# Fire attention in a 12-stage transformer kernel: scores in four 32-row products, projections beside a double-buffered bias stage

## The chip, the cores and the metric

The kernel runs on one core of one Trainium2 chip, as one program. The metric is device time in microseconds from start to end of the execution. Three runs of the kernel before gave 4412.99, 4416.31 and 4423.09 us; their median, 4416.31, is what the change is compared with.

## The reference

The input is 8 sequences of 256 positions and 128 channels. The program puts it through a mixture of experts, a gated recurrence, a second mixture of experts, a 6-layer local transformer, an attention with a position bias called Fire, and a second 6-layer local transformer, each behind a layer normalisation. Only the Fire attention changes. Cut to what it computes, with 16 heads of 8 channels:

```
pos = arange(T);  rel = pos[:, None] - pos[None, :]
pos_norm = log(|c * max(pos, |L| * 512)| + 1) + 1e-6
nd   = log(|c * rel| + 1) / pos_norm[:, None]                    # T x T distances
bias = einsum('tsw,wh->hts', relu(nd[..., None] * w1[0] + b1), w2) + b2   # 32 hidden, 16 heads
bias = where(causal, bias, -inf)
q, k, v = split(x @ Wqkv + bqkv)                                 # 16 heads of 8
att  = softmax(q @ k.T / sqrt(8) + bias)
y    = (att @ v) @ Wproj + bproj;   x = x + y
```

The bias is one table of 16 x 256 x 256 for all 8 sequences.

## The kernel before

`fire_attention_phase` is written with one instruction list for each engine, and semaphores between them; nothing reorders the work, so that an engine takes its list in the order written. It has three blocks, and each ends for all engines before the next begins.

*Setup* (L1364 to L1399): loads of the weights, the relative positions and the like, and the logarithms and the reciprocal that the distances need.

*Bias stage* (L1402 to L1466): the table is made in eight rounds of 32 key positions. A round has eight distance products on DVE (L1416, into `fa_nd`), one Relu of 128x2048 on ACT (L1440, into `fa_hb`), 16 matmuls of 64 columns on PE (L1451; 8 in rounds 4 to 7, where only the second half of the queries can see the keys), and the evacuation with `b2` on DVE (L1424, into `fa_bias`). There is one `fa_nd`, one `fa_hb` and one set of PSUM banks, so that each step of a round waits for the one before. Behind the eighth round GpSimd fills the future positions with -1e30 (L1462).

*Attention* (from L1517): each of the 8 sequences (`b`, two of them in a pass of the loop, told apart by `par`) is split into 12 blocks of 128 queries x 512 columns: four blocks for the first 128 queries (four heads of 128 keys each) and eight for the second 128 (two heads of 256 keys each). 96 blocks run through a pipeline in slots. For a block, PE makes the scores (L1568), DVE adds the bias (L1654) and takes the maximum of a row (L1657), GpSimd subtracts it (L1532), ACT takes the exponential (L1617), PE turns the block by four transposes (L1558), ACT copies it out of PSUM (L1611), and PE weighs the values (L1594). At the end of a tile of 128 queries (after block 4 and block 12) DVE divides by the sum (L1663, L1666), PE turns the result (L1581), ACT copies it (L1621), PE projects it (L1575), ACT adds the bias into `fa_ysb` (L1626) and DVE adds it to `M` (L1673).

Heads have 8 channels, while a matmul contracts over all 128 partitions. The kernel before keeps the keys in `fa_kz`, 16 copies of them, in copy h all channels but those of head h at zero. The copies are made on DVE, four heads at a time (L1643), out of the projection that PE makes at the start of each sequence (L1546, L1550), from a copy of `XN` that GpSimd makes (L1526).

A matmul of float32 shows in the trace as two weight loads (PEld) and two records on PE; a transpose shows as one.

Of the kernel before, what the change touches and what calls it, by code (L numbers as in the profile page):

```python
# [1315 lines left out]
def fire_attention_phase(nc, res, d, M, XN):  # L1316
# [3 lines left out]
    GA, GT = 12, 4  # L1320
    RM = T + 4 * (T // 4 - 1)
    ROFF = RM - T
    with ExitStack() as ctx:
# [16 lines left out]
        hmask = sb("fa_hmask", [P, NH])  # L1340
        rel = sb("fa_rel", [P, RM])
        pn = sb("fa_pn", [P, T])
        nd = sb("fa_nd", [P, 8, T])
        hb = sb("fa_hb", [P, 8, T])
        bias = [sb("fa_bias0", [P, NH, P]), sb("fa_bias1", [P, NH, T])]
        xb = sb("fa_xb", [P, T])
        qT = sb("fa_qT", [P, 2, T])
        kz = sb("fa_kz", [P, 2, NH, T])
        vv = sb("fa_vv", [P, 2, 2, NH, HV])
        S = sb("fa_S", [P, 4, 512])  # L1350
        mx = sb("fa_mx", [P, 4, 4])
        pT = sb("fa_pT", [P, 2, 4, P])
        rd = sb("fa_rd", [P, 2, NH])
        on = sb("fa_on", [P, 2, P])
        oT = sb("fa_oT", [P, P])
        ysb = sb("fa_ysb", [P, 2, P])
        ld, zd, ach, vch = sem("fa_ld"), sem("fa_zd"), sem("fa_ach"), sem("fa_vch")
        ndd, hd_, bp, be = sem("fa_ndd"), sem("fa_hd"), sem("fa_bp"), sem("fa_be")
        SCALE = float(np.float32(1.0) / np.sqrt(np.float32(HD)))


        with nc.Block() as block:
            @block.sync
            def _(sp):  # L1364
                for dst, src in ((wqkv[:, :], d["fa_wqkv"]), (wp[:, :], d["fa_wp"]), (bqk[:, :], d["fa_bqk"]),
                                 (bv[:, :], d["fa_bv"].to_broadcast([P, P])), (b2[:, :], d["fa_b2"].to_broadcast([P, NH])),
                                 (sc[:, 0:2], d["fa_sc"].to_broadcast([P, 2])), (wb[:, :], d["fa_wb"]),
                                 (hmask[:, :], d["c_hmask"]), (rel[:, :], d["c_rel"]), (pn[:, :], d["c_pos"])):
                    sp.dma_start(dst, src).then_inc(ld, 16)
# [5 lines left out]
            @block.gpsimd  # L1375
            def _(pool):
                nc.gpsimd.memset(w2[:, :], 0.0).then_inc(zd, 1)
                nc.gpsimd.memset(vv[:, :, :, :, :], 1.0)
# [21 lines left out]


        with nc.Block() as block:  # L1402
            def rounds(eng, body):
                body(0, 2)
                with eng.Fori(1, 4) as r:
                    body(r, 2)
                with eng.Fori(4, 8) as r:
                    body(r, 1)

            @block.vector  # L1410
            def _(dve):
                def distances(r, tiles):
                    if not isinstance(r, int):
                        dve.wait_ge(hd_, r)
                    for i in range(8):
                        ins = nc.vector.tensor_tensor(nd[:, i, :], rel[:, bass.ds(r * -32 + (ROFF - 4 * i), T)]  # L1416
                                                      if not isinstance(r, int) else rel[:, ROFF - 4 * i:ROFF - 4 * i + T],
                                                      pn[:, :], ALU.mult)
                    ins.then_inc(ndd, 1)

                def evacuate(r, tiles):
                    dve.wait_ge(bp, r + 1)
                    for t in range(2 - tiles, 2):
                        ins = nc.vector.tensor_tensor(bias[t][:, :, bass.ds(r * 32, 32)],  # L1424
                                                      bank[t][:, :].rearrange("p (s h) -> p h s", h=NH),
# [3 lines left out]
                def body(r, tiles):  # L1429
                    distances(r, tiles)  # L1430
                    evacuate(r, tiles)
                rounds(dve, body)

            @block.scalar
            def _(act):
                def body(r, tiles):
                    act.wait_ge(ndd, r + 1)
                    if not isinstance(r, int):
                        act.wait_ge(bp, r)
                    nc.scalar.activation(hb[:, :, :], nd[:, :, :], ACT.Relu, scale=wb[:, 0:1], bias=wb[:, 1:2]).then_inc(hd_, 1)  # L1440
                rounds(act, body)

            @block.tensor
            def _(pe):
                def body(r, tiles):
                    pe.wait_ge(hd_, r + 1)
                    if not isinstance(r, int):
                        pe.wait_ge(be, r)
                    for t in range(2 - tiles, 2):
                        for i in range(8):  # L1450
                            ins = nc.tensor.matmul(bank[t][:, i * 4 * NH:(i + 1) * 4 * NH], hb[:, i, t * P:(t + 1) * P],  # L1451
                                                   w2[:, :], start=True, stop=True, skip_group_check=True)
                    ins.then_inc(bp, 1)
                rounds(pe, body)

            @block.gpsimd
            def _(pool):

                pool.wait_ge(be, 8)
                for t in range(2):  # L1460
                    n = (t + 1) * P
                    nc.gpsimd.affine_select(out=bias[t][:, :, :], in_=bias[t][:, :, :], compare_op=ALU.is_ge, fill=-BIG,  # L1462
                                            base=t * P, pattern=[[0, NH], [-1, n]], channel_multiplier=1)

        simd, addd, mxd, subd, expd = [sem("fa_" + n) for n in ("simd", "addd", "mxd", "subd", "expd")]
        ptT, ptE, pvd = [sem("fa_" + n) for n in ("ptT", "ptE", "pvd")]
        xbd, projd, qE, kzd, vE = [sem("fa_" + n) for n in ("xbd", "projd", "qE", "kzd", "vE")]
        rdd, ond, oTd, oTe, yd, yE, upd = [sem("fa_" + n) for n in ("rdd", "ond", "oTd", "oTe", "yd", "yE", "upd")]  # L1470
        SIM, PTR, PVS, OTR, YPR = 4, 6, 7, 8, 9
        G2 = 2 * GA

        def back(g, k):

# [349 lines left out]
```

## Time and profile before

| | us |
|---|---|
| median of 3 runs | 4416.31 |
| the profiled execution | 4419.39 |
| its span in the trace | 4417.6 |
| PE, DVE, ACT, POOL busy in the span | 3899.8, 3447.6, 3176.4, 2673.5 |
| Fire attention: setup | 12.8 |
| Fire attention: bias stage | 97.2 |
| Fire attention: attention | 299.2 |

The engines are PE (TensorE's matmuls), PEld (its weight loads), DVE (VectorE), ACT (ScalarE), POOL (GpSimd) and SP (SyncE, which starts transfers). [...] Most of the span belongs to the two local transformers (slices 7 to 20 and 26 to 39 of the page's 40). The Fire attention lies between 2307 and 2716 us of the span. The page's chain of waits covers only the last layer normalisation, so that the stage is read from windows and from the timeline.

### The profile page before, as it was taken

How to read it: one execution, taken by the hardware profiler on the slowest of the kernel's cores; microseconds unless marked ns; L12 is line 12 of the kernel's file. 1: busy time of each engine (PE TensorE's matmuls, PEld its weight loads, DVE VectorE, ACT ScalarE, POOL GpSimd, SP SyncE). 2: the span in 40 equal slices, each digit the busy share in tenths (PEclk: the TensorE clock that was granted, in tenths of full speed). 3: DMA queues.
4: the chain of work that ended last, by engine and by line, in shares of the span. 5: the costliest groups of instructions: out<-in, count | busy, mean ns of one | idle time of the engine just before them, and what ended most of it. 6: DMA issues, size and time to landing. Idle time of an engine off the chain costs nothing. (4 is left out here: it accounts for less than half of the span.)

```text
span 4417.6 us, 164417 instructions
## 1 busy us (share of the span) xinstructions
PE 3899.8 (88%) x64144; PEld 2853.1 (65%) x64144; DVE 3447.6 (78%) x6675; ACT 3176.4 (72%) x10347; POOL 2673.5 (61%) x2507
## 2 busy tenths in 40 slices
PE   7966968999999999999954896899999999999996
PEld 3423437777777777777734664777777777777773
DVE  1132129999999999999943664999999999999994
ACT  3343337888888888888841433788888888888884
POOL 1110127777777777777710332777777777877772
PEclk8987989999999999999975987999999999999997
DMA  1101113333333333333310000333333333333341
GB/s 58 57 15 44 57 47 105 115 103 119 100 116 103 106 112 108 114 97 109 117 29 0 1 0 33 103 112 104 119 99 116 104 108 112 103 117 98 106 119 37
DMA packets 549303, 377.81 MB, mean 86 GB/s; under 512 B 32576, under 2 KB 533056, under 8 KB 546240
## 3 DMA queue, kind: packets, MB, share of 16 engines
q1 hardware_dynamic: 548560, 367.57, 27.6%
q8 instruction: 507, 8.31, 0.8%
q14 instruction: 236, 1.93, 0.1%
HBM read 265.37 MB, written 102.11 MB: 83 GB/s over the span
## 5 line engine op out<-in xcount | busy, mean ns | idle before, releaser
L1266 POOL TENSOR_TENSOR lt_t<-lt_t 128x512 f32<-128x512 f32 x768 | 973.5, 1289 | 567.8 <-DVE lt_t L1100 567.8
L1002 ACT ACTIVATE lt_pb<-lt_pb,lt_mx 128x64 f32<-128x64 f32 x3072 | 1023.5, 346 | 0.0
L1272 POOL TENSOR_TENSOR lt_t<-lt_t,lt_rn 128x512 f32<-128x512 f32 x768 | 810.8, 1076 | 118.4 <-DVE lt_rn L1128 117.1
L49 PE MATMUL ps<-lt_wh,lt_xh 128*128 128x512 f32 (+1 forms) x1536 | 581.8, 379 | 148.9 <-DVE lt_t L1100 87.6
L1002 ACT ACTIVATION_READ_ACCUMULATOR lt_pb<-lt_pb,lt_mx 128x1 f32 x3072 | 610.2, 199 | 0.0
L984 ACT ACTIVATE lt_qkT<-ps 128x512 f32<-128x512 f32 x768 | 459.0, 598 | 197.2 <-PE ps L804 196.8
L1111 DVE TENSOR_REDUCE lt_ss<-lt_sq 128x8 f32<-128x512 f32 x768 | 518.7, 675 | 14.5 <-ACT lt_sq L979 9.9
L1100 DVE TENSOR_TENSOR lt_t<-ps,lt_tab 128x512 f32<-128x512 f32 x768 | 522.9, 681 | 2.9
L51 PE MATMUL ps<-lt_wh,lt_xl 128*128 128x512 f32 (+1 forms) x1536 | 523.7, 341 | 0.0
L1106 DVE TENSOR_TENSOR lt_t<-ps,lt_tab 128x512 f32<-128x512 f32 x768 | 521.6, 679 | 1.6 <-PE ps L804 0.3
L50 PE MATMUL ps<-lt_wl,lt_xh 128*128 128x512 f32 (+1 forms) x1536 | 522.8, 340 | 0.0
L804 PE MATMUL ps<-ident,lt_t 128*128 128x128 f32 x3072 | 482.8, 280 | 34.1 <-ACT lt_qkT L984 25.5
L979 ACT ACTIVATE lt_sq<-ps 128x512 f32<-128x512 f32 x768 | 452.8, 590 | 71.4 <-PE ps L51 70.5
L49 PEld LDWEIGHTS ps<-lt_wh,lt_xh 128*128 128x128 f32 x1536 | 290.5, 189 | 267.5 <-issue 150.6
L804 PEld LDWEIGHTS ps<-ident,lt_t 128*128 128x128 f32 x3072 | 355.9, 141 | 159.0 <-issue 105.6
L862 PEld LDWEIGHTS ps<-lt_pT,lt_vw 64*64 64x64 f32 x24576 | 397.1, 135 | 89.0 <-issue 88.7
L862 PE MATMUL ps<-lt_pT,lt_vw 64*64 64x32 f32 x24576 | 439.0, 221 | 4.1 <-issue 3.9
L1278 POOL TENSOR_TENSOR lt_pb<-lt_pb,lt_rd 128x512 f32<-128x512 f32 x384 | 400.8, 1044 | 34.1 <-DVE lt_rd L1145 30.7
L876 PE MATMUL ps<-lt_oT,lt_wo 128*128 128x256 f32 x1536 | 405.1, 386 | 1.8 <-ACT lt_oT L1014 1.4
L372 POOL TENSOR_TENSOR M<-M,moe_tmp 128x512 f32<-128x512 f32 x64 | 81.0, 1266 | 510.5 <-DVE moe_tmp L354 510.5
L354 DVE SCALAR_TENSOR_TENSOR moe_tmp<-ps,moe_bb,moe_cbc 128x512 f32<-128x512 f32 x64 | 48.1, 751 | 419.8 <-PE ps L306 419.8
L832 PEld LDWEIGHTS ps<-lt_qkT 64*32 64x32 f32 x24576 | 271.1, 105 | 139.1 <-issue 136.7
(196 smaller groups left out, 7989.3 us busy)
## 6 DMA issues: line engine op xcount, KB each, us to landing
lt_vw<-v_scratch SPq DMA_DIRECT2D x768, 256.0 KB, 3.7
v_scratch<-lt_vv SPq DMA_DIRECT2D x384, 256.0 KB, 2.1
lt_wraw<-in_lt_wqkv SPq DMA_DIRECT2D x56, 384.0 KB, 5.6
moe_cbc<-comb_scratch SPq DMA_DIRECT2D x16, 1024.0 KB, 6.7
moe_w<-in_moe_w SPq DMA_DIRECT2D x32, 256.0 KB, 2.8
lt_wo<-in_lt_wo SPq DMA_DIRECT2D x48, 128.0 KB, 3.7
lt_w<-in_lt_w SPq DMA_DIRECT2D x12, 341.0 KB, 4.2
lt_w<-in_lt_w SPq DMA_DIRECT2D x12, 192.0 KB, 3.3
```

The source lines that it names most:

```text
L49: nc.tensor.matmul(out, lh, rh, start=start, stop=False)
L50: nc.tensor.matmul(out, lh, rl, start=False, stop=False)
L51: return nc.tensor.matmul(out, ll, rh, start=False, stop=stop)
L804: ins = nc.tensor.transpose(TB[:, q * P:(q + 1) * P], t1[:, u[1] % 2, t, q * P:(q + 1) * P], ident[:, :])
L862: ins = nc.tensor.matmul(OR[r][64 * e:64 * e + 64, t * P + w * WIN:t * P + w * WIN + WIN], vw[h, k, 4 * t + w, e * DH:(e + 1) * DH], pT[h, ...
L984: nc.scalar.activation(qkT[:, u[1] % 2, :, WIN + t * P:WIN + (t + 1) * P], TB.rearrange("p (a n) -> p a n", a=4), ACT.Copy).then_inc(tE[t], 1)
L1002: ins = nc.scalar.activation(p, p, ACT.Exp, bias=mx[:, par, c:c + 1], accum_out=sm[:, par, c:c + 1])
L1100: nc.vector.tensor_tensor(o4, a4[:, :, :, ::-1, :], s4, ALU.mult).then_inc(rotd[t], 1)
L1106: nc.vector.tensor_tensor(t1[:, u[1] % 2, t, :].rearrange("p (w h c) -> p w h c", w=2, c=DH), A[t][:, :].rearrange("p (w h c) -> p w h c", ...
L1111: nc.vector.tensor_reduce(ss[:, u[1] % 2, 8 * t:8 * t + 8], sq[:, t, :].rearrange("p (h c) -> p h c", c=DH), AX.X, ALU.add).then_inc(ssd[t ...
L1266: nc.gpsimd.tensor_tensor(o, o, t2[:, t, :], ALU.add).then_inc(padd[t], 1)
L1272: nc.gpsimd.tensor_tensor(o, o, rn[:, u[1] % 2, 8 * t:8 * t + 8].unsqueeze(2).to_broadcast([P, 8, DH]), ALU.mult).then_inc(qkd[t], 1)
```

## The change

*Heads by groups of 32 rows.* Channels 32r to 32r+31 hold the heads 4r to 4r+3. `fa_kz` now has four copies for each sequence, each with one head of every group of 32 partitions. A product of 32 rows (`scores`, L1560) then gives the scores of the heads of one group; the four of a group of blocks use the four quarters of the array's rows and write banks 0 to 3. Blocks are numbered so that the row group runs fastest; in one group of four blocks, each block has another r. DVE adds the bias of the four blocks one after the other, and then takes the maximum of one block in each slot. `fa_S` has 8 buffers, `fa_pT` 3, and the PSUM banks of the turned weights and of the output move.

*Projections.* All eight sequences are projected in the bias stage, one in each round, straight from `XN`, ahead of the round's products on PE. ACT copies the queries and the keys (`take_queries`), DVE the values, and GpSimd spreads the keys (`spread_keys`). Queries, keys and values of all sequences are kept.

*Bias stage.* `fa_nd`, `fa_hb` and the PSUM banks of the products have two buffers. The causal fill is made in each round for its 32 positions.

*Loops.* All loops are written out, so that waits are on constants.

The diff, cut to its core:

```diff
@@ bias stage @@
+                distances(0)
+                for r in range(8):
+                    if r < 7:
+                        distances(r + 1)
+                    take_values(r)
+                    take_bias(r)
...
             @block.scalar
             def _(act):
-                def body(r, tiles):
-                    act.wait_ge(ndd, r + 1)
-                    if not isinstance(r, int):
-                        act.wait_ge(bp, r)
-                    nc.scalar.activation(hb[:, :, :], nd[:, :, :], ACT.Relu, scale=wb[:, 0:1], bias=wb[:, 1:2]).then_inc(hd_, 1)
-                rounds(act, body)
+                def hidden(r):
+                    act.wait_ge(ndd, r + 1)
+                    if r >= 2:
+                        act.wait_ge(bp, r - 1)
+                    nc.scalar.activation(hb[:, r % 2, :, :], nd[:, r % 2, :, :], ACT.Relu, scale=wb[:, 0:1],
+                                         bias=wb[:, 1:2]).then_inc(hd_, 1)
+
+                def take_queries(b):
+                    act.wait_ge(qkp, b + 1)
+                    nc.scalar.activation(qT[:, b, :], bank[4 + b % 2][:, 0:T], ACT.Identity, bias=sc[:, 3:4],
+                                         scale=SCALE).then_inc(qE, 1)
+                    if b >= 2:
+                        act.wait_ge(kzd, b - 1)
+                    nc.scalar.activation(kT[:, b % 2, :], bank[4 + b % 2][:, T:2 * T], ACT.Identity, bias=bqk[:, 1:2]).then_inc(kE, 1)
+                for r in range(8):
+                    take_queries(r)
+                    hidden(r)
...
+                for r in range(8):
+                    project(r)
+                    biases(r)
...
+                def spread_keys(b):
+                    pool.wait_ge(kE, b + 1)
+                    nc.gpsimd.tensor_tensor(kz[:, b, :, :], kT[:, b % 2, :].unsqueeze(1).to_broadcast([P, GR, T]),
+                                            hmask[:, :].unsqueeze(2).to_broadcast([P, GR, T]), ALU.mult).then_inc(kzd, 1)
@@ attention, PE @@
-                        nc.tensor.matmul(bank[q[1] % 2][:, :].rearrange("p (h k) -> p h k", h=nh),
-                                         qT[:, par, t * P:(t + 1) * P], kz[:, par, h0:h0 + nh, 0:nk],
-                                         start=True, stop=True).then_inc(simd, 1)
+                def scores(q):
+                    if q:
+                        pe.wait_ge(addd, q)
+                    for r in range(GR):
+                        b, _, t, a, nh, nk = info(q + r)
+                        rows = slice(32 * r, 32 * r + 32)
+                        nc.tensor.matmul(bank[r][:, :].rearrange("p (h k) -> p h k", h=nh),
+                                         qT[rows, b, t * P:(t + 1) * P], kz[rows, b, a:a + nh, 0:nk],
+                                         start=True, stop=True).then_inc(simd, 1)
...
+                def slot(n):
+                    q = at(n, PTR)
+                    if q is not None:
+                        turn_weights(q)
+                    q = at(n, SIM)
+                    if q is not None and q % GR == 0:
+                        scores(q)
+                    tl = tile_end(at(n, YPR))
+                    if tl is not None:
+                        project(tl)
+                    tl = tile_end(at(n, OTR))
+                    if tl is not None:
+                        turn_output(tl)
+                    q = at(n, PVS)
+                    if q is not None:
+                        weigh(q)
@@ attention, DVE @@
+                def slot(n):
+                    q = at(n, SIM)
+                    if q is not None:
+                        if q % GR == 0:
+                            for k in range(GR):
+                                add_bias(q + k)
+                        maximum(q)
+                    q = at(n, PVS)
+                    tl = tile_end(q)
+                    if tl is not None:
+                        take_output(q, tl)
+                    tl = tile_end(at(n, YPR))
+                    if tl is not None:
+                        update(tl)
```

The lags are, in slots behind the scores (`SIM`): turning (`PTR`) 2, weighing (`PVS`) 3, turning of the output (`OTR`) 4, its projection and the update of M (`YPR`) 5; between these stages they were the same before.

On ACT, in the bias stage, the rows before are these (the Relu of round 0, of the rounds 1 to 3 in a loop, of 4 to 7 in a loop, and then the first rows of the attention):

```order
L1440 ACTIVATE fa_hb<-fa_nd,fa_wb 128x2048
L1405 UNCONDITIONAL_BRANCH
L1405 ISA
L1440 ACTIVATE fa_hb<-fa_nd,fa_wb 128x2048
L1405 REGISTER_ALU
L1405 COMPARE_AND_BRANCH
```

and after the change (`fa_qT` the queries, `fa_kT` the keys, `fa_hb` the Relu):

```order
L1453 ACTIVATE fa_qT<-ps,fa_sc 128x256
L1457 ACTIVATE fa_kT<-ps,fa_bqk 128x256
L1448 ACTIVATE fa_hb<-fa_nd,fa_wb 128x2048
L1453 ACTIVATE fa_qT<-ps,fa_sc 128x256
L1457 ACTIVATE fa_kT<-ps,fa_bqk 128x256
L1448 ACTIVATE fa_hb<-fa_nd,fa_wb 128x2048
```

The copies of a sequence's queries and keys, which stood at its start in the attention (L1605), now stand ahead of the Relu of each round.

On PE, in the attention, before (turned weights `fa_S`, scores from `fa_kz` and `fa_qT`, weighing of `fa_vv`; the first two rows end a block):

```order
L1558 MATMUL ps<-ident,fa_S 128x128 x4
L1568 MATMUL ps<-fa_kz,fa_qT 128x512
L1594 MATMUL ps<-fa_vv,fa_pT 128x10 x4
L1558 MATMUL ps<-ident,fa_S 128x128 x4
L1568 MATMUL ps<-fa_kz,fa_qT 128x512
L1594 MATMUL ps<-fa_vv,fa_pT 128x10 x4
```

and after the change, from one group's scores to the next:

```order
L1560 MATMUL ps<-fa_kz,fa_qT 128x512 x4
L1583 MATMUL ps<-fa_vv,fa_pT 128x10 x4
L1551 MATMUL ps<-ident,fa_S 128x128 x4
L1583 MATMUL ps<-fa_vv,fa_pT 128x10 x4
L1551 MATMUL ps<-ident,fa_S 128x128 x4
L1583 MATMUL ps<-fa_vv,fa_pT 128x10 x4
L1551 MATMUL ps<-ident,fa_S 128x128 x4
L1583 MATMUL ps<-fa_vv,fa_pT 128x10 x4
L1551 MATMUL ps<-ident,fa_S 128x128 x4
L1560 MATMUL ps<-fa_kz,fa_qT 128x512 x4
```

The scores of every block stand together at the head of a group of four; of the four turnings between two scores rows, the first belongs to the last block of the group before, and the last to the third block of the group.

On DVE, in the attention, before (bias addition `fa_S`, maximum `fa_mx`, and the two instructions that divide the output):

```order
L1654 TENSOR_TENSOR fa_S<-ps,fa_bias_10 128x512
L1657 TENSOR_REDUCE fa_mx<-fa_S 128x2
L1663 RECIPROCAL fa_rd<-ps 128x16
L1666 TENSOR_TENSOR fa_on<-ps,fa_rd 128x128
L1654 TENSOR_TENSOR fa_S<-ps,fa_bias_10 128x512
L1657 TENSOR_REDUCE fa_mx<-fa_S 128x2
L1654 TENSOR_TENSOR fa_S<-ps,fa_bias_10 128x512
L1657 TENSOR_REDUCE fa_mx<-fa_S 128x2
L1673 TENSOR_TENSOR M<-M,fa_ysb 128x128
```

and after the change, two groups:

```order
L1643 TENSOR_TENSOR fa_S<-ps,fa_bias_10 128x512 x4
L1650 TENSOR_REDUCE fa_mx<-fa_S 128x2
L1665 TENSOR_TENSOR M<-M,fa_ysb 128x128
L1650 TENSOR_REDUCE fa_mx<-fa_S 128x2 x3
L1643 TENSOR_TENSOR fa_S<-ps,fa_bias_10 128x512 x4
L1650 TENSOR_REDUCE fa_mx<-fa_S 128x4 x3
L1655 RECIPROCAL fa_rd<-ps 128x16
L1659 TENSOR_TENSOR fa_on<-ps,fa_rd 128x128
L1650 TENSOR_REDUCE fa_mx<-fa_S 128x4
```

The update of M stands between the first and the second maximum of a group, and the division of the output between the third and the fourth.

## Rows read from the trace of the kernel before

**Rows 1.** Windows of the Fire stages: span, length, busy us (count) by engine, PEclk

```profile
2320.02:2417.26 97.24, 43.05 (x192) 41.55 (x192) 29.45 (x76) 16.74 (x8) 5.68 (x3) 0.50 0.00 0
2417.26:2716.48 299.22, 265.75 (x1456) 197.68 (x1456) 182.53 (x280) 118.03 (x232) 102.54 (x104) 0.88 0.00 0
2430.60:2530.00 99.40, 87.95 (x548) 66.45 (x547) 68.76 (x105) 43.93 (x86) 38.44 (x39) 1.00 0.00 1
...
2611.50:2625.00 13.50, 13.50 (x46) 9.73 (x45) 4.97 (x9) 4.15 (x9) 3.46 (x4) 0.50 0.00 0
```

**Rows 2.** Timeline, bias stage: start us, us, engine, instruction, idle before

```profile
2338.25 7.09 PE L1451 MATMUL ps<-fa_w,fa_hb 128*128 128x64 f32 x32 [6.19 <-ACT fa_hb L1440]
2345.49 1.29 DVE L1424 TENSOR_TENSOR fa_bias<-ps,fa_b 128x512 f32 x2 [9.41 <-PE ps L1451]
...
2349.49 2.09 ACT L1440 ACTIVATE fa_hb<-fa_nd,fa_wb 128x2048 f32<-128x2048 f32 x1 [11.29 <-DVE fa_nd L1416]
...
2351.64 7.09 PE L1451 MATMUL ps<-fa_w,fa_hb 128*128 128x64 f32 x32 [6.29 <-ACT fa_hb L1440]
...
2406.53 3.67 PE L1451 MATMUL ps<-fa_w,fa_hb 128*128 128x64 f32 x16 [5.70 <-ACT fa_hb L1440]
```

**Rows 3.** Timeline, end of the bias stage and start of the attention

```profile
2411.28 5.67 POOL L1462 TENSOR_SCALAR_AFFINE_SELECT fa_bias<-fa_bias 128x2048 f32<-128x2048 f32 x2 [103.30 <-DVEq L1402]
2417.26 0.40 POOL L1526 COPY fa_xb<-XN 128x256 f32<-128x256 f32 x1 [0.30 <-SPq L1518]
...
2417.70 2.07 PE L1546 MATMUL ps<-fa_xb,fa_wqkv 128*128 128x256 f32 x4 [7.50 <-POOL fa_xb L1526]
...
2419.82 0.47 ACT L1605 ACTIVATE fa_qT<-ps,fa_sc 128x256 f32<-128x256 f32 x1 [13.35 <-PE ps L1546]
```

**Rows 4.** Timeline, a block from maximum to turning

```profile
2425.30 0.69 DVE L1657 TENSOR_REDUCE fa_mx<-fa_S 128x4 f32<-128x512 f32 x1
...
2426.07 1.04 POOL L1532 TENSOR_TENSOR fa_S<-fa_S,fa_mx 128x512 f32<-128x512 f32 x1 [8.42 <-DVE fa_mx L1657]
...
2427.15 0.63 ACT L1617 ACTIVATE fa_S<-fa_S 128x512 f32<-128x512 f32 x1 [6.86 <-POOL fa_S L1532]
...
2427.83 1.12 PE L1558 MATMUL ps<-ident,fa_S 128*128 128x128 f32 x4 [1.70 <-ACT fa_S L1617]
```

**Rows 5.** Timeline of PE alone, a tile end and a block at full clock

```profile
2501.39 0.49 PE L1575 MATMUL ps<-fa_oT,fa_wp 128*128 128x128 f32 x2 [1.16 <-ACT fa_oT L1621]
...
2505.14 1.02 PE L1568 MATMUL ps<-fa_kz,fa_qT 128*128 128x512 f32 x2
2506.00 0.96 PE L1594 MATMUL ps<-fa_vv,fa_pT 128*128 128x10 f32 x8
```

**Rows 6.** Timeline, a block at half the clock

```profile
2613.68 1.09 PE L1558 MATMUL ps<-ident,fa_S 128*128 128x128 f32 x4
...
2614.57 1.91 PE L1568 MATMUL ps<-fa_kz,fa_qT 128*128 128x512 f32 x2
...
2616.27 1.72 PE L1594 MATMUL ps<-fa_vv,fa_pT 128*128 128x10 f32 x8
...
2616.52 0.69 DVE L1654 TENSOR_TENSOR fa_S<-ps,fa_bias 128x512 f32<-128x512 f32 x1 [2.75 <-PE ps L1568]
...
2617.84 1.09 PE L1558 MATMUL ps<-ident,fa_S 128*128 128x128 f32 x4
```

**Rows 7.** Timeline, the end of a tile

```profile
2448.20 0.35 ACT L1626 ACTIVATE fa_ysb<-ps,fa_bqk 128x128 f32<-128x128 f32 x1
...
2448.58 0.29 DVE L1673 TENSOR_TENSOR M<-M,fa_ysb 128x128 f32<-128x128 f32 x1 [2.07 <-ACT fa_ysb L1626]
...
2448.79 0.42 DVE L1635 TENSOR_TENSOR fa_vv<-ps,fa_bv 128x256 f32<-128x256 f32 x1
```

**Rows 8.** Timeline of PE in the second local transformer

```profile
2853.49 0.86 PE L832 MATMUL ps<-lt_qkT 64*32 64x64 f32 x64
```

**Rows 9.** Timeline, the last weighing

```profile
2710.13 3.31 PE L1594 MATMUL ps<-fa_vv,fa_pT 128*128 128x10 f32 x16
```

More of the change, by code:

```diff
@@ L1399, in _, with tiles, distances @@
                 nc.vector.reciprocal(pn[:, :], pn[:, :])
+        def tiles(r):
+            return (0, 1) if r < 4 else (1,)
         with nc.Block() as block:
[L1403 to L1408, printed above, removed]
             @block.vector
             def _(dve):
-                def distances(r, tiles):
-                    if not isinstance(r, int):
-                        dve.wait_ge(hd_, r)
+                def distances(r):
+                    if r >= 2:
+                        dve.wait_ge(hd_, r - 1)
@@ L1443, in _, with project @@
+                for r in range(8):
+                    take_queries(r)
+                    hidden(r)
             @block.tensor
             def _(pe):
-                def body(r, tiles):
+                def project(b):
+                    x = XN[:, b * T:(b + 1) * T]
+                    if b >= 2:
+                        pe.wait_ge(kE, b - 1)
+                        pe.wait_ge(vE, b - 1)
+                    for w in range(2):
+                        ins = nc.tensor.matmul(bank[4 + b % 2][:, w * T:(w + 1) * T], wqkv[:, w * P:(w + 1) * P], x,
+                                               start=True, stop=True, skip_group_check=True)
+                    ins.then_inc(qkp, 1)
+                    for t in range(2):
+                        ins = nc.tensor.matmul(bank[6 + b % 2][:, t * P:(t + 1) * P], x[:, t * P:(t + 1) * P], wqkv[:, 2 * P:3 * P],
+                                               start=True, stop=True, skip_group_check=True)
+                    ins.then_inc(vpd, 1)
@@ L1467, in fire_attention_phase @@
[L1467 to L1474, printed above, removed]
-            b, i = g
-            i -= k
-            while i < 0:
-                b, i = b - 1, i + G2
-            return None if isinstance(b, int) and b < 0 else (b, i)
@@ L1487, in info, with at @@
+                for r in range(8):
+                    spread_keys(r)
+                    forget_future(r)
+        SIM, PTR, PVS, OTR, YPR = 0, 2, 3, 4, 5
+        def at(n, k):
+            return n - k if 0 <= n - k < GN else None
         def info(q):
-            par, i = q[1] // GA, q[1] % GA
-            return (par, 0, 4 * i, 4, P) if i < GT else (par, 1, 2 * (i - GT), 2, T)
+            b, i = divmod(q, GB)
+            part, r = divmod(i, GR)
+            return (b, r, 0, 0, 4, P) if part == 0 else (b, r, 1, 2 * (part - 1), 2, T)
@@ L1513, in at, with stream @@
-        def at(g, k, live):
-            q = back(g, k)
-            return q if q is not None and (live or q[0] == B // 2 - 1 and isinstance(q[0], int)) else None
+            return 2 * (q // GB) + (q % GB == GB - 1)
+        def stream(slot):
+            for n in range(GN + YPR):
+                slot(n)
         with nc.Block() as block:
@@ L1675, in fire_attention_phase @@
+                        update(tl)
+                stream(slot)
         clear(nc, sems)
```

333 lines of the change are left out of this document (138 added, 195 removed).

## The prediction, made before the changed kernel ran

> **What bounds the kernel now.** Windows come first, since the diff touches one of twelve stages and a share over the whole span says nothing of it. The Fire attention spends 97.2 us on the bias tables (2320.02 to 2417.26) and 299.2 us on the attention itself (2417.26 to 2716.48) [rows 1]. Its setup and the other stages run unchanged code, and I cost them at nothing; two more semaphores are cleared at the end, which is below 0.2 us.
>
> In the bias stage the timeline shows one thing at a time: 16 small products (32 records) on PE, the evacuation on DVE, eight distance products on DVE, the Relu on ACT, then PE again 13.4 us after it last began [rows 2]. [...]
>
> In the attention the timeline of a block (one of 96) shows PE at work nearly without a break. At full clock scores take 0.86 us and weighing (L1594) 0.81, its 0.96 less the 0.15 by which neighbouring records overlap [rows 5]; at the half level, 4.16 us go to turning (0.89), scores (1.70) and weighing (1.57) [rows 6]. PE is busy for 265.8 of 299.2 us at a mean clock of 0.88; DVE, ACT and POOL are busy for 183, 118 and 103 [rows 1]. So PE bounds the stage, and the clock that it is granted matters as much as its work.
>
> **Bias stage, part by part.** Two buffers take the distances off the path: they fit in while PE works. But the order on ACT puts the queries' and keys' copies of batch r ahead of the Relu of round r, and PE makes those projections only behind the products of round r-1. So the Relu still can't start while PE works on the round before. From one round's products to the next at the half clock: 32 records issue in 6.83 us (7.09 less the end of the last; 3.41 for the 16 of rounds 4 to 7) [rows 2]; projections until the query copy starts 2.12 [rows 3]; two copies of 128x256, each 0.47 long, pipelined at about 0.38; Relu start to products 2.15 [rows 2]. That is 11.86 us for four periods and 8.44 for three. The first products start at 2324.98 as before (the first projection fits in front of them), so the last start at 2324.98 + 47.4 + 25.3 = 2397.7. From there before took 4.75 us to the causal fill [rows 2, 3], which is now one piece of 512 columns (5.67 us for 6144 [rows 3]: I take 0.7 with its fixed part), and 0.3 to the next stage: 2403.5 in place of 2417.26, **-13.8 us**. GpSimd's spreading of the keys is 128x1024, twice the 1.04 us of the 128x512 one [rows 4], and hides in rounds of over 8 us; if it slowed DVE, DVE has more than 3 us of slack a round.
>
> If the clock rose in this stage the period would be 3.42 + 1.2 + 0.76 + 2.15 = 7.5 us, and 5.8 later: the stage would end at 2376.6, -40.6. Between the ends I take the half clock, since every round has PE idle for over 2 us, and grant 3 us for stretches at the full one after the dense projections: -16.8.
>
> **Attention, part by part.** The projections, the key spreading (32 DVE instructions) and the copies of queries and values leave the rows. Scores come four blocks at a time. The 64 records of 64x64 on parts of the array (L832) take 0.86 us in all [rows 8], where one stream, scaled from a 128x512 record (0.43), would take 64 x 0.053 = 3.4: products on different parts of the array do run side by side. So I take four 32-row products at the time of one, 0.86 us, or 1.70 at the half level.
>
> The new loop is a group of four blocks. DVE adds the bias of all four before the first maximum; PE must turn the third block before the next scores. At the half clock: scores to first add 1.95 [rows 6]; four adds at 0.60 (two take 1.29 [rows 2]) 2.40; maximum to subtraction 0.77, to exponential 1.08, to turning 0.68 [rows 4]: 6.88 us. Then turn, weigh, turn, weigh, turn = 3 x 0.89 + 2 x 1.57 = 5.81, and the next scores: **12.69 us a group**. The other two weighings and the fourth turning (4.03) lie behind the scores inside the 6.88 (1.70 + 4.03 = 5.73): hidden, with 1.15 to spare.
>
> Added waits: the output's update of M stands on DVE between the first and second maximum. It waits for ysb, which ACT makes right behind the exponential (0.63 long [rows 4], 0.54 with the overlap), and comes 0.38 after that begins [rows 7]. Behind it stand three maxima and all that POOL, ACT and PE make of them: the second maximum goes from 4.95 to 7.33, its turning from 9.34 to 9.86, +0.52 in 14 of groups 0 to 22. Turning the output adds 0.21 in 15 of them. The normalisation, which waits for the weighing at 9.34, delays the fourth maximum; it is back before the next group's adds.
>
> Sum: 22 x 12.69 = 279.2, the first group without a weighing 11.3, waits 7.3 + 3.2, start 0.4, and the last group to the end 21.8 (turning and weighing of the last block end at 18.8, the output chain takes the 3.0 left after the 3.31 of the last 16 weighing records [rows 9] before 2716.48): **323.2 against 299.2, +24.0 us**. The 3.4 us of PE that a group saves is there, but at half the clock the rest of PE's work and the chain of 6.88 fill more than it frees.
>
> The same at the full clock: 1.95 less 0.85 to the add, chain 6.0, turnings 0.49 (half of 0.89 and a little that doesn't scale), weighings 0.81: 9.1 us, 10.8 where the update waits (1.7 more, since less PE work hides it), 254 us in all: -45.
>
> **Which clock.** In the attention PE had 1.00 from 2430.6 to 2530 while it streamed 512 columns twice in every block and waited 1.2 us at the ends of tiles [rows 1, 5]; it still fell to 0.50 in short stretches such as 2611.5 to 2625, in which it was busy without a break [rows 1]. In the new loop at full clock it would work 5.8 us of 9.1 and be idle for 3 in one piece, in which it now waits for the chain. That is closer to the bias stage (7 us of work, 6 of waiting, 0.50 all through [rows 1, 2]) than to the old block. I take 0.50 for nearly the whole stage. The clock may rise behind a scores product, but there PE has slack: it would gain nothing.
>
> [...]
>
> [...]
>
> **Sum.** 4419.4 (the profiled execution) + 24.0 - 16.8 = 4426.6. The median of the runs is 3.1 below the profiled one: **4424 us**, +8, or 0.2% slower.
>
> **Rivals.**
> 1. *The clock stays up* (faster). Attention -45 and bias -17 to -41: 4330 to 4355; if it is up for half the time, 4380. For it: PE did hold 1.00 with waits at every tile end. Against it: the idle 3 us in every group. The point from which it decides is whether PE still has the full clock when it starts the three turnings. Chance 0.22.
> 2. *The four products don't fully overlap* (slower). A product is two records; if the second must wait for the first in order, only neighbours overlap, and scores take 5 x 0.85 = 4.26 us at the half clock. Then PE is free at 8.3 in place of 6.88: +1.4 to 1.8 a group, 24 groups, +40: 4464. Entirely in series, 6.8 us a group would give +100, unless the denser PE gets the clock back, when it is -26. For it: no product in this trace has 32 rows and 128 columns. Against it: L832's two records a product have the same order and reach over four at a time. It decides once scores last longer than 2.85 us. Chance 0.15.
> 3. *The bias stage overlaps after all*, with attention as forecast: 4400. That needs the Relu ahead of the copies, which the order excludes; it is inside the bounds above.
>
> **How the numbers follow.** Forecast 0.63, its own range 4408 to 4440 (0.3 us a group either way, and 5 for the bias stage); rival 1 0.22; rival 2 0.15. The change can't be told from none within 0.2%, that is 4407.5 to 4425.1. From the forecast come 0.04 faster, 0.29 same, 0.30 slower; from rival 1 0.19 and 0.03; from rival 2 0.15 slower. Faster 0.23, same 0.32, slower 0.45. The range 4378 to 4466 leaves out the clock held at full throughout and the serial product.
>
> **What would show it.** Right: PEclk near 0.5 to 0.6 over the attention; groups of scores 12.7 to 13.4 us apart; in the bias stage PE idle about 2 us between projections and products, products 11.9 us apart, then 8.4; the update of M waiting about 2 us on ACT. Wrong: a clock of 0.9 in the attention with groups at 9 to 11 us (rival 1); scores of four that last over 2.9 us at the half clock, or DVE waiting between its four adds (rival 2); rounds of the bias under 8 us from the start.

## The result, and the profile after

The changed kernel takes **4424.89 us** (median of 20 runs, 4417.14 to 4434.82), the kernel before 4416.50 (20 runs, 4408.51 to 4425.43): a ratio of **1.0018, 95% interval 1.0011 to 1.0026**. The interval leaves out 1, so the change made the kernel slower, though by only some 0.2%. The forecast was 4424.0. The profiled execution spans 4422.9 us against 4417.6.

The windows of the bias stage and the attention after the change (length, busy us and count on PE, PEld, DVE, ACT and POOL, granted clock, DMA share, GB/s), and 100 us of the attention; they answer to [rows 1]. The granted clock (PEclk) is TensorE's, as a share of the full one. In this trace it has two levels: of 2200 stretches of 0.2 us, one every 2 us of the span, 1845 show 1.00 and 348 show 0.50; the other seven lie between. A level named "half" or "full" below is one of these.

```profile
2324.09:2403.87 79.78, 60.73 (x256) 55.58 (x257) 45.44 (x84) 22.54 (x24) 24.73 (x16) 0.59 0.00 1
2403.87:2733.50 329.63, 299.16 (x1392) 249.15 (x1392) 130.04 (x240) 115.82 (x224) 98.00 (x96) 0.53 0.00 1
2480.00:2580.00 100.00, 95.72 (x440) 79.45 (x439) 39.44 (x73) 35.35 (x68) 28.84 (x29) 0.51 0.00 1
```

The bias stage fell from 97.2 to 79.8 us (-17.4) although it now holds all projections. The attention rose from 299.2 to 329.6 (+30.4), and its clock fell from 0.88 to 0.53: PE is busy for 33 us longer with less work. The two make +13.0; the spans differ by 5.3 and the medians by 8.4, since the unchanged stages differ between any two profiled executions: what stands ahead of the bias stage took 4.1 us more (it begins at 2324.09 against 2320.02, and at 2317.26 in one of the runs below), and what follows the attention 11.7 us less (1689.4 against 1701.1).

A round of the bias stage after the change, as timelines give it (start us, us, engine, instruction, idle before), beside [rows 2]:

```profile
2335.93 2.02 PE L1470 MATMUL ps<-XN,fa_wqkv 128*128 128x256 f32 x4
...
2337.38 4.97 DVE L1418 TENSOR_TENSOR fa_nd<-fa_rel,fa_pn 128x256 f32<-128x256 f32 x8
2337.69 1.02 POOL L1503 TENSOR_SCALAR_AFFINE_SELECT fa_bias<-fa_bias 128x512 f32<-128x512 f32 x1 [6.40 <-DVE fa_bias L1424]
...
2337.99 0.47 ACT L1453 ACTIVATE fa_qT<-ps,fa_sc 128x256 f32<-128x256 f32 x1 [8.99 <-PE ps L1470]
2338.36 0.47 ACT L1457 ACTIVATE fa_kT<-ps,fa_bqk 128x256 f32<-128x256 f32 x1
2338.71 2.09 ACT L1448 ACTIVATE fa_hb<-fa_nd,fa_wb 128x2048 f32<-128x2048 f32 x1
2338.91 2.15 POOL L1496 TENSOR_TENSOR fa_kz<-fa_kT,fa_hmask 128x1024 f32<-128x1024 f32 x1 [0.20 <-ACT fa_kT L1457]
```

The products of rounds 0, 1 and 4, a timeline of PE:

```profile
2329.04 7.09 PE L1484 MATMUL ps<-fa_w,fa_hb 128*128 128x64 f32 x32 [2.06 <-ACT fa_hb L1448]
2340.86 7.09 PE L1484 MATMUL ps<-fa_w,fa_hb 128*128 128x64 f32 x32 [2.06 <-ACT fa_hb L1448]
...
2375.76 2.42 PE L1484 MATMUL ps<-fa_w,fa_hb 128*128 128x64 f32 x16 [2.06 <-ACT fa_hb L1448]
```

The Relu still starts behind the copies, PE waits 2.06 to 2.40 us for it in every round, and rounds are 11.8 us apart (one 11.3), then 7.1 to 8.0 (some of them at a higher clock for a part: round 4 takes 2.42 us of products in place of 3.68).

A group of four blocks in the attention (from the scores at 2482.46 to those at 2495.65), and of the next group the update of M (2502.91) and its end at 2509.34:

```profile
2482.46 0.52 PEld L1560 LDWEIGHTS ps<-fa_kz,fa_qT 32*128 32x128 f32 x8 [0.33 <-issue]
2482.46 2.09 PE L1560 MATMUL ps<-fa_kz,fa_qT 32*128 32x512 f32 x8
...
2484.48 1.78 PEld L1583 LDWEIGHTS ps<-fa_vv,fa_pT 128*128 128x128 f32 x8 [1.50 <-issue]
2484.49 1.88 PE L1583 MATMUL ps<-fa_vv,fa_pT 128*128 128x10 f32 x8
2484.57 2.48 DVE L1643 TENSOR_TENSOR fa_S<-ps,fa_bias 128x512 f32<-128x512 f32 x4 [6.26 <-PE ps L1560]
...
2486.97 1.86 DVE L1650 TENSOR_REDUCE fa_mx<-fa_S 128x4 f32<-128x512 f32 x3
...
2487.73 3.03 POOL L1540 TENSOR_TENSOR fa_S<-fa_S,fa_mx 128x512 f32<-128x512 f32 x3 [7.49 <-DVE fa_mx L1650]
2488.80 0.63 ACT L1619 ACTIVATE fa_S<-fa_S 128x512 f32<-128x512 f32 x1 [5.63 <-POOL fa_S L1540]
...
2489.49 1.11 PE L1551 MATMUL ps<-ident,fa_S 128*128 128x128 f32 x4 [0.67 <-ACT fa_S L1619]
...
2494.63 1.09 PE L1551 MATMUL ps<-ident,fa_S 128*128 128x128 f32 x4
...
2495.65 2.09 PE L1560 MATMUL ps<-fa_kz,fa_qT 32*128 32x512 f32 x8
...
2502.91 0.29 DVE L1665 TENSOR_TENSOR M<-M,fa_ysb 128x128 f32<-128x128 f32 x1 [2.07 <-ACT fa_ysb L1631]
...
2509.34 2.09 PE L1560 MATMUL ps<-fa_kz,fa_qT 32*128 32x512 f32 x8
```

Scores of groups are 13.19 us apart where an output is turned in the group, 13.48 where M is updated (2468.98 to 2482.46), and 13.69 where both happen. The four products together take 2.03 us, up to the weighing behind them. PE waits only 0.67 us here for the chain add, maximum, subtraction, exponential; the rest of the group is half-clock work. The two PEld rows are weight loads: at both ends of the scores the next load starts only with its own matmul.

### The profile page after: what moved, and what is told of

The parts are those of the page before. It is cut to its first block and busy times, and to the rows that moved or that the text cites. A ratio compares the mean times of both kernels' runs of the same rounds, so it can differ in the third digit from the quotient of the medians.

```text
span 4422.9 us, 163782 instructions
## 1 busy us (share of the span) xinstructions
PE 3945.8 (89%) x64144; PEld 2914.3 (66%) x64144; DVE 3410.0 (77%) x6643; ACT 3179.8 (72%) x10355; POOL 2689.4 (61%) x2513
## 3 DMA queue, kind: packets, MB, share of 16 engines
q14 instruction: 238, 1.95, 0.2%
## 5 line engine op out<-in xcount | busy, mean ns | idle before, releaser
L979 ACT ACTIVATE lt_sq<-ps 128x512 f32<-128x512 f32 x768 | 452.5, 589 | 69.3 <-PE ps L51 68.6
```

## Experiments

Each is an edit of the changed kernel; its ratio is to the kernel before, run on the same chip, so the changed kernel is 1.0018 on this scale; differences between runs go by these ratios, to a few us. The diffs are cut to their core.

**one_by_one: the same 32-row products, one a block.**

```diff
-for r in range(GR):                # four products, once in four slots
+if q >= GR: pe.wait_ge(addd, q - GR + 1)
+b, r, t, a, nh, nk = info(q)       # one product, in every slot
-if q is not None and q % GR == 0: scores(q)
+if q is not None: scores(q)
```

(On DVE each block is added just ahead of its maximum.)

> The changed kernel with the grouping undone and all else kept: each block's scores are one product of 32 rows in its own slot, with its bias addition behind it, still in four banks. Theory: PE streams 512 columns in every block again, the clock returns to about that of before (0.88), a block takes 2.2 to 2.8 us and the attention 250 to 285 us: 4350 to 4380. Rival (four products side by side are the gain, and the clock stays at 0.50 with four times the score time): a block takes 4.2 to 4.5 us and the attention over 400: 4500 or more.

4561.68 us, ratio 1.0343 (1.0324 to 1.0362): the rival's time. PE's timeline, and the window of the attention:

```profile
2503.09 2.07 PE L1559 MATMUL ps<-fa_kz,fa_qT 32*128 32x512 f32 x2
2505.09 1.88 PE L1582 MATMUL ps<-fa_vv,fa_pT 128*128 128x10 f32 x8
2506.82 1.09 PE L1551 MATMUL ps<-ident,fa_S 128*128 128x128 f32 x4
2507.85 2.07 PE L1559 MATMUL ps<-fa_kz,fa_qT 32*128 32x512 f32 x2
```

```profile
2392.25:2860.52 468.27, 463.24 (x1392) 288.57 (x1392) 145.60 (x240) 114.21 (x224) 99.81 (x96) 0.50 0.00 0
```

PE is busy for 463 of 468 us, streams 512 columns in every block, and stays at 0.50. One product takes 2.00 us, as four together took 2.03: in the changed kernel the four overlap fully. And with 5 us of idle in the whole stage the clock is at its lower level: idle time is not needed to hold it there.

**rows128: one_by_one with products over all 128 rows.** Its scores mix four heads; nothing else differs.

```diff
-rows = slice(32 * r, 32 * r + 32)
+rows = slice(0, P)
```

> The kernel with one scores product a block (one_by_one), but the product contracts over all 128 rows instead of 32: the same number of products, of columns and of waits, four times the rows. Its scores then mix four heads, so the output is not the attention's. Theory (a product of 32 rows does little for TensorE's clock, whatever its columns): the clock of the attention stage returns to 0.85 or more, a block takes 2.3 to 3.1 us instead of 4.75, and the time falls from 4561.7 to 4340-4420. Rival (the clock follows the columns streamed or TensorE's busy share, and stays low for another reason of the new order): clock 0.50, a block 4.7 us, 4555-4570.

4370.85 us, ratio 0.9901 (0.9875 to 0.9928). PE's timeline and the window of the attention:

```profile
2508.67 1.02 PE L1559 MATMUL ps<-fa_kz,fa_qT 128*128 128x512 f32 x2
2509.53 0.96 PE L1582 MATMUL ps<-fa_vv,fa_pT 128*128 128x10 f32 x8
2510.34 0.63 PE L1551 MATMUL ps<-ident,fa_S 128*128 128x128 f32 x4
2510.81 1.02 PE L1559 MATMUL ps<-fa_kz,fa_qT 128*128 128x512 f32 x2
```

```profile
2397.20:2664.02 266.82, 234.42 (x1392) 173.51 (x1392) 144.15 (x240) 114.17 (x224) 99.76 (x96) 0.95 0.00 1
```

The same number of products and columns, four times the rows: clock 0.95 in place of 0.50, a block that waits for nothing 2.14 us in place of 4.75, and the kernel some 190 us less. The rows of the scores products decide which level this loop gets.

**group128: the changed kernel's groups of four, 128 rows** (the same edit of the rows; the scores mix four heads again).

> The changed kernel with its groups of four kept, but each of the four products over all 128 rows (its scores mix four heads, so the output is not the attention's). Theory (rows decide the clock, the grouping does no harm of its own): clock 0.9 or more; four products take 4 x 0.86 = 3.4 us in place of 2.0 to 2.1, hidden behind the adds and the chain; group 9 to 9.6 us, 10.8 where M is updated; attention 245-262 us and the time 4345-4360, which is below rows128. Rival (the long idle piece once a group keeps the clock down as well): clock 0.6 or below, group 14-17 us, 4440-4500.

4445.67 us, ratio 1.0070 (1.0049 to 1.0090). The time is the rival's; the clock is neither 0.9 or more nor 0.6 or below, but 0.73. A group in PE's timeline, and the window of the attention:

```profile
2503.39 1.12 PE L1551 MATMUL ps<-ident,fa_S 128*128 128x128 f32 x4 [1.16 <-ACT fa_S L1619]
...
2504.51 1.72 PE L1583 MATMUL ps<-fa_vv,fa_pT 128*128 128x10 f32 x8
2506.08 1.09 PE L1551 MATMUL ps<-ident,fa_S 128*128 128x128 f32 x4
2506.97 4.96 PE L1560 MATMUL ps<-fa_kz,fa_qT 128*128 128x512 f32 x8
...
2511.99 0.96 PE L1583 MATMUL ps<-fa_vv,fa_pT 128*128 128x10 f32 x8
2512.80 0.64 PE L1551 MATMUL ps<-ident,fa_S 128*128 128x128 f32 x4
```

```profile
2393.70:2745.67 351.97, 308.44 (x1392) 226.01 (x1392) 136.79 (x240) 114.10 (x224) 97.91 (x96) 0.73 0.00 1
```

The clock swings once a group: half (weighing 1.72, turning 1.09) up to the scores, full from within them (weighing 0.96, turning 0.64), half again by the end of the small products. The four scores products begin at the half level and cost 4.8 us. With rows128 this fills a square of four:

| scores products | one a block | four together |
|---|---|---|
| 32 rows | clock 0.50, attention 468 us, ratio 1.0343 | 0.53, 330 us, 1.0018 |
| 128 rows | 0.95, 267 us, 0.9901 | 0.73, 352 us, 1.0070 |

So the clock of this loop is lower in two cases: with products of 32 rows (0.50 and 0.53), and, where the products have 128 rows, with four of them together (0.73 against 0.95), be it for the bunching or for the wait that comes with it. With 32 rows it is at or near its lower level in either order. Overlap pays for most of it (468 to 330), but the old form needed no such pay.

**warm3: three products of 128 rows and 512 columns a group, never read,** ahead of the first turning:

```diff
 def turn_weights(q):
+    if q % GR == 0:
+        pe.wait_ge(addd, q + 1)
+        for _ in range(3):
+            nc.tensor.matmul(bank[0][:, :], ident[:, :], XN[:, 0:512], ...)
     pe.wait_ge(expd, q + 1)
```

> The changed kernel with work added: ahead of the first turning of each group of four blocks, where PE is idle, three products of 128x512 float32 into a score bank that has been read, whose result nobody uses. Theory (the clock holds the stage back: PE's idle stretch between its bursts takes it to 0.50): the clock rises to near 1.00 over the attention, groups come every 9 to 11 us in place of 13.2, the attention takes 255 to 270 us in place of 329.5, and the kernel 4355 to 4370 us, although it does 72 products more. Rival (the chain from scores to turning and PE's own work set the pace, the clock is a by-product): the added products cost 5.1 us a group at half the clock, of which about 1 is hidden: +95 us, 4520.

4401.29 us, ratio 0.9971 (0.9958 to 0.9983): right in sign, about a third of the size (some 21 us below the changed kernel, where 55 to 70 were expected). The attention's window:

```profile
2397.10:2700.35 303.25, 286.61 (x1536) 199.64 (x1536) 129.98 (x240) 113.21 (x224) 97.80 (x96) 0.80 0.00 1
```

More work on the engine that bounds the stage made it 26 us shorter (303.3 against 329.6). The clock was up for part of the time only: groups at the full level came 9.8 and 11.0 us apart, as the theory said (2503.25 to 2513.09, and to 2524.10), others up to 14.7.

**deep: turning and all behind it two slots later,** so that four blocks still wait to be turned while PE makes the scores of a group, and PE need not wait for the chain:

```diff
-SIM, PTR, PVS, OTR, YPR = 0, 2, 3, 4, 5
+SIM, PTR, PVS, OTR, YPR = 0, 4, 5, 6, 7
```

> The changed kernel, with turning, weighing and the tile's end two slots later (4, 5, 6, 7 behind the scores instead of 2, 3, 4, 5), so that TensorE computes the scores of a group while four blocks still wait to be turned. Theory (TensorE waits for the chain add, maximum, subtraction, exponent once a group, and nearly all else is half clock): the idle 30 us of the stage go, the clock stays at 0.5-0.6, group 12.3-12.6 us, time 4385-4400. Rival A (the idle is what holds the clock down): with no idle the clock rises, group 8-9 us, time 4300-4330. Rival B (the wait only moves to the update or the copies of ScalarE): 4415-4425.

4428.88 us, ratio 1.0026 (1.0010 to 1.0042): nothing gained. PE's timeline (a group from scores to scores) and the attention's window:

```profile
2513.44 2.09 PE L1560 MATMUL ps<-fa_kz,fa_qT 32*128 32x512 f32 x8
2515.47 1.88 PE L1583 MATMUL ps<-fa_vv,fa_pT 128*128 128x10 f32 x8
2517.19 1.09 PE L1551 MATMUL ps<-ident,fa_S 128*128 128x128 f32 x4
...
2526.15 2.09 PE L1560 MATMUL ps<-fa_kz,fa_qT 32*128 32x512 f32 x8
```

```profile
2397.63:2729.93 332.30, 300.90 (x1392) 248.03 (x1392) 128.65 (x240) 115.72 (x224) 98.01 (x96) 0.53 0.00 1
```

A group in which PE waits 0.21 us in all still lasts 12.71 us at the half level; the group before it, which turns an output, 13.92, with 0.89 of waiting for the division. Right behind the group shown the clock rose for a moment (weighing 1.21 us, turning 0.63), and PE then waited 2.01 us for the division, so that nothing came of it. The chain was worth under 1 us a group, and the wait came back at the turning of the output (18.7 us in 16) and in the longer start and end. Rival A, that the clock rises once the idle goes, is out: in this the theory held, though its 4385 to 4400 did not. What happened is rival B, the wait moved, at 4 us above its range.

**relu_first: the Relu ahead of the copies in the bias stage.**

```diff
 for r in range(8):
+    hidden(r)
     take_queries(r)
-    hidden(r)
```

> The changed kernel with one exchange: in the bias stage ACT makes the Relu of a round before it copies the queries and keys of that round. Theory (the copies, behind the projections, keep the Relu from starting while PE works on the round before): PE goes from round to round without a pause, 9.7 us at half the clock and 6.3 in the late rounds, so that the stage takes 66 us in place of 79.8, and if the dense work brings the full clock, 45 to 50: 4395 to 4411 us. Rival (the Relu waits for something else, the distances or a buffer): no change, 4425.

4403.54 us, ratio 0.9977 (0.9966 to 0.9987), so 18 us below the changed kernel. The first products to the first scores take 53.0 us (2322.20 to 2375.18) in place of 74.9, and the attention behind is the same, 329.4. The order on ACT was the bound of the bias stage. Part of the 22 us is the clock, which rose with it (0.74 over the stage, against 0.59). **deep_relu** has both edits:

> deep and the Relu ahead of the copies of queries and keys in the bias stage. Theory: the two add up, 15-19 us below deep, 4368-4385. Rival (the clock at the end of the bias stage decides how the attention starts, so that they don't add): within 5 us of deep, or over 30 below it.

4408.68 us, ratio 0.9983 (0.9971 to 0.9994): 20 below deep. They add up, but from deep's higher base, so that the time itself was missed.

**update_late: the update of M two slots later on DVE** (`update(tile_end(at(n, YPR + 2)))`).

> The changed kernel with the update of M moved on DVE from between the first and second maximum of a group to behind the third. Theory: 14 groups lose 0.5 us of waiting, the attention is 7 us shorter: 4418 us. Rival (PE is the bound at half the clock and hides the late maximum): no change, 4425.

4416.37 us, ratio 1.0010 (1.0000 to 1.0019): some 3.5 us less than the changed kernel, with intervals that overlap, so that the times alone make it only likely. The traces are clearer. From the second scores to the last the changed kernel takes 295.67 us (2415.44 to 2711.11), this one 288.54 (2412.15 to 2700.69): 7.1 us less, as the theory said. A group with an update alone now takes 12.98 us in place of 13.48, one with both 13.18 in place of 13.69. The waits of the adds for scores fell from 123.8 to 117.4 us in 24.

**deep_warm: deep_relu and the three products of warm3.**

> deep_relu with three products of 128 rows and 512 columns more in each group of four blocks (their result is never read). Theory (128-row products hold the clock up): attention clock 0.9 or more, group 8-9.5 us, time 4285-4325. Rival (TensorE is full already, the three only cost 3 x 0.43 us at half clock or more a group with the clock unchanged): 4400-4440.

4489.10 us, ratio 1.0170 (1.0143 to 1.0198): the largest miss. PE's timeline:

```profile
2515.49 4.95 PE L1550 MATMUL ps<-XN,ident 128*128 128x512 f32 x6
2520.27 0.60 PE L1555 MATMUL ps<-ident,fa_S 128*128 128x128 f32 x4
2520.80 1.14 PE L1564 MATMUL ps<-fa_kz,fa_qT 32*128 32x512 f32 x8
...
2527.36 1.88 PE L1587 MATMUL ps<-fa_vv,fa_pT 128*128 128x10 f32 x8 [2.65 <-ACT fa_pT L1617]
```

Here the three stand right beside the scores, all large products in one bunch: they run mostly at the half level (4.8 us up to the turning, where 2.7 were read in warm3), the clock rises behind them, while PE soon waits, and is at half again when the weighings resume. In warm3 the three stood 3.5 us behind one group's scores and 7.5 us ahead of the next (2513.09, 2516.58, 2524.10). It looks like group128's swing; the longer wait here (2.65 us) stands as a rival that no run separates.

**masked3: the best version.** The queries of each row group go into a zeroed copy of their own, so that one product over 128 rows gives one block's scores exactly; one a block; the Relu first; turning, weighing and the tile's end at 3, 4, 6 and 8 slots.

```diff
-qT = sb("fa_qT", [P, B, T])
+qT = sb("fa_qT", [P, B, GR, T])     # zeroed by GpSimd in the setup
-nc.scalar.activation(qT[:, b, :], bank[4 + b % 2][:, 0:T], ...)
+for r in range(GR):
+    rows = slice(32 * r, 32 * r + 32)
+    nc.scalar.activation(qT[rows, b, r, :], bank[4 + b % 2][rows, 0:T], ...)
-qT[rows, b, t * P:(t + 1) * P], kz[rows, b, a:a + nh, 0:nk]
+qT[:, b, r, t * P:(t + 1) * P], kz[:, b, a:a + nh, 0:nk]
-SIM, PTR, PVS, OTR, YPR = 0, 2, 3, 4, 5
+SIM, PTR, PVS, OTR, YPR = 0, 3, 4, 6, 8
```

> As masked, with turning, weighing and the tile's end one slot later (3, 4, 6, 8), so that TensorE no longer waits 0.35 us for the exponent in every second block. Theory: masked less 5 to 15 us, 4318-4345. Rival (TensorE is full, nothing gained): within 3 us of masked.

**4329.12 us, ratio 0.9803 (0.9785 to 0.9821)**: 87 us below the kernel before and some 95 below the changed one. Nearly half of the 87 is the bias stage, 53.9 us (2324.33 to 2378.26) where it was 97.2; the attention is 47.8 shorter. **masked**, with 2, 3, 5 and 7 slots:

> All of the attention is computed, with 128-row scores: ScalarE writes the queries of each of the four row groups into a zeroed copy of their own, so that one product a block over all 128 rows gives that block's scores (as rows128, now exact). With it the Relu ahead of the copies, turning of the output at 5 and projection and update at 7 slots behind instead of 4 and 5. Theory (rows decide the clock, and what is left in rows128 is the wait of the projection of 1.2 us in each of 16 tiles and the order of ScalarE in the bias stage): 4371 less 17 (Relu) less 10 to 19 (waits of the tile's end), plus up to 9 us for zeroing on GpSimd and 8 x 1 us for the four copies: 4330-4355. Rival (zeroing and the copies lie in the open and the clock of the bias stage falls): 4365-4385.

4344.45 us, ratio 0.9840 (0.9824 to 0.9857). Both as expected. **masked_group** is masked3 with the groups of four:

> As masked3 (128-row scores from zeroed copies of the queries, Relu first, lags 3, 4, 6, 8), but with the groups of four of the changed kernel. All of the attention is computed. Theory: TensorE's work a group is the same as masked3's four blocks, and its idle comes in one piece of under 1 us: within 10 us of masked3, 4322-4340. Rival (grouping costs more than the row size): above 4360.

4393.70 us, ratio 0.9950 (0.9931 to 0.9970). The rival held: only the grouping of the products and of their adds differs, and it costs 65 us. The attention's windows of masked3 and of masked_group:

```profile
2378.26:2629.64 251.38, 232.97 (x1392) 173.75 (x1392) 142.47 (x240) 114.28 (x224) 99.95 (x96) 0.93 0.00 1
```

```profile
2373.43:2696.43 323.00, 294.66 (x1392) 216.24 (x1392) 136.12 (x240) 111.26 (x224) 96.77 (x96) 0.75 0.00 1
```

Is it the bunching, or the wait that PE has once a group? A wait does stand where the clock falls, as PE's timeline of masked_group shows:

```profile
2509.40 1.19 PE L1586 MATMUL ps<-fa_vv,fa_pT 128*128 128x10 f32 x8 [0.96 <-ACT fa_pT L1616]
2510.44 1.09 PE L1555 MATMUL ps<-ident,fa_S 128*128 128x128 f32 x4
```

But waits of that size don't do it by themselves. In rows128 PE waited up to 1.2 us in each of 16 tiles and mostly 0.35 in 32 places more, 33.5 us in all, at a clock of 0.95; masked_group waited 29.8 us in all, 1.1 at the longest but for the start, at 0.75. What the bunching does without any wait, no run with 128 rows shows.

## Why the prediction was right, step by step

- **Time.** 4424.0 forecast, 4424.89 measured. From the end of the last update of M to the next stage's first product the trace has 2.56 us before and 2.70 after, 0.14 us more, where the prediction put the two more semaphores below 0.2. Part of the agreement is luck: the attention came out 6.4 us dearer, and the unchanged stages of the profiled execution 8 us cheaper, for which nothing is known but their spread from execution to execution.
- **Bias stage, -16.8.** Measured -17.4. The order on ACT, the 11.86 and 8.44 us and the short clock rises were as described (11.8; 7.1 to 8.0, the first to the last products 69.3 us where 72.8 less 3 was forecast), and relu_first shows the cause. Causal fill 0.72 in place of 0.7.
- **Chain.** 0.77, 1.08, 0.68 forecast; 0.76, 1.07, 0.69 read.
- **Four products at the time of one.** Confirmed by one_by_one (2.00 for one, 2.03 for four). Rival 2 is out.
- **Group 12.69, +0.21, +0.52: the mis-sized term.** Turning the output alone gives 12.90 forecast, 13.19 read; with the update 13.42 and 13.69. The missing 0.27 to 0.29 a group, over 24 groups 6.5 us, is the whole excess of the stage (+30.4 against +24.0). It sits at both ends of the scores: 1.02 us from the turning to the scores where full-size products take 0.89, also inside group128 (2506.08 to 2506.97), and 2.11 from scores to the first add, not 1.95. That is 0.13 and 0.16, together 0.29. update_late bears it out: with the update's wait gone, a group that turns no output takes 12.98. The products themselves last 2.00 to 2.03 in place of 1.70, and the weighing behind them 1.72 in place of 1.57; what of this is more than 0.16 is hidden in the group. Two weight loads mark the places: elsewhere in the group a load starts some 0.2 us ahead of its first matmul (2486.00 for the turning at 2486.21), there not (2482.46, 2484.48). The forecast has no term for such a gap, and 24 x 0.29 is 7 us. In the traces it stands where 32-row products meet full-size ones (no gap of 0.13 in group128, where all have full size; at both ends the loads don't run ahead); what makes it was not tested.
- **Clock 0.50 nearly throughout.** Measured 0.53. The level was right, its reason wrong. That 3 us of idle in one piece a group bring the half level was the author's estimate, by the likeness to the bias stage. In the trace PE waits 0.7 us there, and one_by_one (5 us of idle in 468, 0.50) and deep (a group with 0.21 of waiting, still 12.71 us) show that idle did not set it; rows128 (0.95) puts it on the 32 rows; what grouping takes from 128-row products in group128 (0.95 to 0.73) had little left to take here (0.50 one a block, 0.53 in groups).
- **The idle itself.** The prediction's own sum left 1.15 us of it a group at the half clock (0.67 read, or 0.82 counted as the prediction counts; the products and the weighing behind them take 0.48 more, the chain 0.15); its argument on the clock took the 3 us of the full level, in a loop that reached that level for short stretches only.
- **Rival 1** (0.22) asked for the full clock at the three turnings. It never had it. In five groups (2576.36 to 2633) the clock rose behind the scores (weighing 0.96 to 1.20 us and turning 0.64, where the half level takes 1.72 and 1.09), as the prediction held possible, and they took 13.2 to 13.7 us as the others: PE then waited 2.1 to 2.5 us for the chain, the slack that the prediction spoke of. warm3 shows what part of it was worth: -26 us of attention at 0.80. rows128 came within its 4330 to 4380, but by another change: full rows, without the overlap.
- **Update of M.** 2.07 us of waiting in 15 tiles (31.1 us in all), as forecast. 14 x 0.52 = 7.3 us had been charged for it, and moving it gave 7.1 in the trace (3.5 by the times, whose intervals allow either).

What stays open: why 32-row products do not bring the clock up, even when four of them run side by side (0.53), was not separated further, nor whether bunched 128-row products lower it without a wait; and what makes the 0.13 and 0.16 us at the two ends of the 32-row products was not measured.

## What to carry to other kernels

Before packing small contractions side by side, ask what the large products do for the clock: the four products saved some 2.6 us of PE a group at the full level (four at 0.86 [rows 5] in the time of one), and nearly all of PE's work then ran at half (0.53 over the stage, 0.88 before). Spread full-height products evenly among small ones rather than collecting them (0.93 in masked3, 0.75 in masked_group), and pad a short contraction with zeros if nothing else keeps the clock up; here that, with the projections moved out, made the attention 16% shorter than before the change (251.4 us against 299.2), which had padded keys and a clock of 0.88 already. Where a copy and the operation that feeds the bounding engine stand on one queue, put the feeding one first (relu_first: 53.0 us in place of 74.9).

## What the runs showed of the hardware

- The granted clock of one loop with equal counts of products and columns was 0.50 with 32-row and 0.95 with 128-row scores, and 0.95 against 0.73 (128 rows, one a block against four together) by their order and the waits that come with it.
- DVE took longer beside GpSimd. Eight distance products of 128x256 took 2.76 us before the change, and 4.97 after it (the row at 2337.38 above), while GpSimd filled and spread for 1.02 and 2.15 us. DVE had the slack (busy for 45.4 of the stage's 79.8 us; each Relu stood behind ACT's copies, not behind the distances), so it cost nothing here. The timeline of the kernel before:

```profile
2346.69 2.76 DVE L1416 TENSOR_TENSOR fa_nd<-fa_rel,fa_pn 128x256 f32<-128x256 f32 x8
```

- GpSimd can be the one that takes longer: its first spreading, begun beside DVE's first sixteen products, took 4.20 us, later ones 2.15 and 1.89. DVE lost nothing there (5.46 us for sixteen), and the spreading ended 1.74 us after they did. The timeline of the changed kernel:

```profile
2324.09 5.46 DVE L1418 TENSOR_TENSOR fa_nd<-fa_rel,fa_pn 128x256 f32<-128x256 f32 x16 [0.30 <-PEq L1367]
...
2327.09 4.20 POOL L1496 TENSOR_TENSOR fa_kz<-fa_kT,fa_hmask 128x1024 f32<-128x1024 f32 x1 [12.86 <-ACT fa_kT L1457]
```
